# Two-layer pre-activation convolution: dense 3x3 stage, sixteen rounds behind it, seven chunk slots for x, two tile buffers

## What is computed

```
x = x + L0(groupnorm(x))      # layer 0
x = x + L1(groupnorm(x))      # layer 1

L0:  f    = relu(Wc @ x + bc)                        # 1x1, 512 -> 128 channels
     g    = relu(mean(x) @ Wc.T + bc) (x) Wkk + bkk  # 3x3 kernel from the means
     sk   = relu(Wc @ max over the 3x3 cells(x) + bc)
     dynW = relu(Wck[:, 0] * g + Wck[:, 1] * sk + bck)   # 128x128 channels, per image
     y    = conv3x3(f, dynW) + b_ad                  # 128 -> 128
     out  = Wf @ y + bf                              # 1x1, 128 -> 512 channels
L1:  grouped 3x3 convolution, 32 groups of 16 channels, no bias
```

## Time and profile before

| | us |
|---|---|
| device time, median of 3 runs | 3925.79 (3924.04 to 3929.71) |
| profiled execution, device time | 3910.82 |
| span of the profiled execution | 3909.1 |
| stage A of image 1 starts, of image 31 starts | 134.03, 3710.69 |
| mean granted TensorE clock | 0.970 |
| PE, DVE, ACT, POOL busy | 3543.0 (91%), 3003.4 (77%), 2177.4 (56%), 990.5 (25%) |
| DRAM traffic | 810.21 MB at 207 GB/s |

### The profile page before, as it was taken

One profiled execution on the slowest core, in us unless ns is written; L12 is line 12 of the kernel. 1 busy time (PEld: TensorE's weight loads), 2 busy tenths in 40 slices (PEclk: granted clock), 3 DMA queues, 4 the chain that ended last, 5 costly groups with the idle time before them and its releaser, 6 DMA issues.

```text
span 3909.1 us, 64944 instructions
## 1 busy us (share of the span) xinstructions
PE 3543.0 (91%) x18048; PEld 2728.8 (70%) x18048; DVE 3003.4 (77%) x8020; ACT 2177.4 (56%) x3911; POOL 990.5 (25%) x1036
## 2 busy tenths in 40 slices
PE   5799999999999999998999999999999999999996
PEld 4577776677776777766677767777666777667775
DVE  7788787778787878877787778787777877787853
ACT  4465555665555664556655556655566555566554
POOL 2131222322222322223222123222232131232223
PEclk9899999999999999999999999999999999999998
DMA  5778667777667786668776687866686776778646
GB/s 101 216 217 233 203 187 217 231 228 221 190 197 226 224 231 210 184 193 236 223 229 198 181 227 224 237 212 183 187 249 209 229 211 179 220 220 238 204 112 173
DMA packets 389593, 810.21 MB, mean 207 GB/s; under 512 B 67250, under 2 KB 297012, under 8 KB 376756
## 3 DMA queue, kind: packets, MB, share of 16 engines
q1 hardware_dynamic: 375220, 658.76, 61.2%
q10 hardware_dynamic: 14336, 151.00, 11.0%
HBM read 501.40 MB, written 308.28 MB: 207 GB/s over the span
## 4 chain that ended last, share of the span: by engine, by line
issue 65%; POOL 21%; PE 6%; DVE 3%; DMA 3%; SPq 1%; POOLq 1%; ACT 1%; ACTq 0%; DVEq 0%
POOL hl L410 21%; DMA tb<-x_rows 1%; PE pd L910 1%; PE pb L910 1%; PE pd L911 1%; PE pd L912 1%; PE pb L912 1%; PE pb L911 1%; POOLq L409 1%; DVE bst L636 1%; DVE mx L638 1%; DMA out<-tb 1%; DMA tb<-x 1%; DMA x_rows<-mrow 0%; PE pac L910 0%
## 5 line engine op out<-in xcount | busy, mean ns | idle before, releaser
L410 POOL TENSOR_TENSOR hl<-un,hl 128x384 f16<-128x384 f32 x1024 | 962.9, 942 | 2838.1 <-ACT hl L435 2838.0
L910 PE MATMUL pd<-hl,k_h 128*96 128x384 f16 x3072 | 1043.6, 340 | 220.0 <-POOL hl L410 135.5
L911 PE MATMUL pd<-hl,k_h 128*96 128x384 f16 x3072 | 1036.1, 337 | 0.0
L912 PE MATMUL pd<-hl,k_l 128*96 128x384 f16 x3072 | 1034.5, 337 | 0.0
L821 DVE SCALAR_TENSOR_TENSOR tb<-pd,kout,tb 96x384 f32<-96x384 f32 x1024 | 621.8, 607 | 327.7 <-PE pd L912 321.2
L431 ACT ACTIVATE un<-tb,b_t,s_t 128x384 f32<-128x384 f32 x1024 | 710.2, 694 | 153.8 <-DMA tb<-x_rows 147.1
L435 ACT ACTIVATE hl<-un 128x384 f16<-128x384 f32 x1024 | 538.8, 526 | 298.6 <-PE pd L912 269.5
L910 PEld LDWEIGHTS pd<-hl,k_h 128*96 128x96 f16 x3072 | 388.6, 126 | 418.7 <-issue 192.8
L810 DVE SCALAR_TENSOR_TENSOR x1b<-pac,bfc,xb 128x288 f32<-128x288 f32 (+2 forms) x1408 | 544.1, 430 | 81.9 <-PE pac L912 76.7
L478 ACT ACTIVATE xs<-pb,badc 128x480 fp32r<-128x480 f32 (+1 forms) x160 | 103.5, 647 | 846.0 <-PE pb L912 846.0
L910 PE MATMUL pb<-fh,dynh 128*128 128x480 f32 (+1 forms) x1440 | 553.3, 384 | 8.2 <-DVE dynl L715 8.2
(11 more groups left out here) (107 smaller groups left out, 4014.7 us busy)
## 6 DMA issues: line engine op xcount, KB each, us to landing
x_rows<-x1b SPq DMA_DIRECT2D x128, 1152.0 KB, 13.9
tb<-x_rows SPq DMA_DIRECT2D x128, 1152.0 KB, 9.6
out<-tb ACTq DMA_DIRECT2D x128, 1152.0 KB, 7.9
tb<-x SPq DMA_DIRECT2D x372, 384.0 KB, 9.7
xb<-x SPq DMA_DIRECT2D x124, 720.0 KB, 6.3
xb<-x SPq DMA_DIRECT2D x124, 432.0 KB, 10.6
tb<-x_rows SPq DMA_DIRECT2D x256, 192.0 KB, 10.7
x_rows<-mrow SPq DMA_DIRECT2D x64, 96.0 KB, 10.0
```

Of the source, the lines that this page charges most:

```text
L410: pool.tensor_tensor(hl[:, g % HL_RING, 1, :, 1:W + 1], un[:, g % U_RING], hl[:, g % HL_RING, 0, :, 1:W + 1], ALU.subtract).then_inc(hl_lo, 1)
L910: pe.matmul(acc, high_w, high_x, start=start, stop=False)
L911: pe.matmul(acc, high_w, low_x, start=False, stop=False)
L912: return pe.matmul(acc, low_w, high_x, start=False, stop=stop)
```

## The change

Stages B and C are taken apart. Per image TensorE runs A, then B without anything between its taps, then 16 rounds. A round is a pair of layer-1 groups of the preceding image (18 matmuls), and in rounds 0 to 5 four C units besides. C is cut otherwise: 24 units, chunk by chunk and row class by row class (a row class is the eight rows that lie six apart, 384 columns), so that x1 of a chunk is complete after six units. The residual has 24 operations, one for a unit. A pair's output is one DVE operation over two banks, 96 x 768; the pairs alternate between the banks pd and pb.

x has seven chunk slots: one for chunk 0, two for each other chunk. Each chunk of x is loaded once, whole; moments and maxima of chunks 1 to 3 are taken during B, of chunk 0 in rounds 3 to 5. x1b holds two chunks, so a chunk's x1 is written to DRAM before the chunk after next is made. tb has two slots, `T_SLOT = [0, 1, 0, 1]`: the load of chunk 2 waits for the store of chunk 0 of the same image, that of chunk 3 for the store of chunk 1. All DMAs, stores too, are issued by SP. ACT takes the squares of x1 in four operations of 2304 elements in place of 12, behind groups 7, 10, 13 and 16. The dynamic weights are made in rounds 13 and 14, with their high part at the end of the image and the low part in A. The loop's body is two images.

The diff, cut to its core:

```diff
-C_AFTER = (2, 4, 6, 8)
-D_FIRST = 13
-EARLY = 3
-LATE = {D_FIRST + 1: (0, 1), D_FIRST + 2: (2, 3)}
...
-AT_X_LOW = (28, 29, 30, 31)
-AT_SCALES = 6
...
-PREP_AT = (5, 6, 7, 8, 9, 11)
-PREP_IN_B = (4, 2)
-PREP_C = (0, 2, 3, 4, 3)
-PREP_FIRST = (0, 0, 1, 2, 3)
...
-STORE_AT = {20: 1, 28: 2}
-TAIL_STORE_AT = {12: 0, 20: 1}
+X_SLOTS = 7
+X1_SLOTS = 2
+T_SLOTS = 2
+T_SLOT = [0, 1, 0, 1]
...
+EARLY = {3: (0, 1), 4: (2, 3)}
+EARLY_GROUPS = 4
+AHEAD = XS_RING
+
+C_ROUNDS = 6
...
+STATS_IN_B = (1, 2, 3)
+STATS_LATE = (0,)
+SQUARE_AFTER = {7: 0, 10: 1, 13: 2, 16: 3}
+ROOT_AFTER = 22
+DYN_LOW_AT = 1
+SCALES_BEFORE = 2
+MOMENTS_AT = {3: (0, 0), 4: (0, 1)}
+MAXIMA_AT = {5: 0}
...
+PREP_MEANS_AT = 7
+PREP_VARIANCES_AT = 9
+PREP_SCALED_AT = 11
...
+def x_slot(c, odd):
+
+    return c if c < 1 else c + 3 * odd
...
+            def load_x(n, odd, c):
+                if isinstance(n, int) and n == 1 and c in STATS_IN_B:
+                    sp.wait_ge(max_done, Q)
+                    sp.wait_ge(k_lo, K_PARTS)
+                elif c in STATS_IN_B:
+                    reached(sp, x1_done, (n - 2) * CUNITS + (c + 1) * OR_)
+                sp.dma_start(xb[:, x_slot(c, odd), :], x_d[n, c]).then_inc(x_in[c], 16)
+            def write_x1(n, c):
+                dst, made = sc_w[n, c, :, :, AT:AT + BW], n * CUNITS + (c + 1) * OR_
+                sp.wait_ge(x1_done, made)
+                sp.dma_start(dst, x1b[:, c % X1_SLOTS]).then_inc(x1_out[c], 16)
...
-            def stage_x(n, pieces):
...
-                    stage_x(n + 1, range(STAGES + 2))
...
+                sp.wait_ge(x1_out[c], written)
...
+                if T_SLOT[c] in T_SLOT[:c]:
+                    sp.wait_ge(stored[T_SLOT.index(T_SLOT[c])], written)
+                else:
+                    reached(sp, stored[Q - 1 - T_SLOT[::-1].index(T_SLOT[c])], free)
...
+            def store(n, c):
+                dst, made = out[n, c], n * PAIRS + (c + 1) * PER_CHUNK
+                sp.wait_ge(out_done, made)
+                sp.dma_start(dst, t_slot(c)[0:M6].rearrange("p j b w -> p (j b w)")).then_inc(stored[c], 16)
...
+            def step(n, odd, d=True, more=True):
+                if d:
+                    if isinstance(n, int) and n == 1:
+                        sp.wait_ge(k_lo, K_PARTS)
+                    for c in range(2):
+                        load_t(n - 1, c)
                 if more:
+                    for c in STATS_IN_B:
+                        load_x(n + 1, 1 - odd, c)
+                for c in range(2):
+                    write_x1(n, c)
+                    if more and c in STATS_LATE:
+                        load_x(n + 1, 1 - odd, c)
+                if d:
+                    store(n - 1, 0)
+                write_x1(n, 2)
                 if d:
                     load_t(n - 1, 2)
+                write_x1(n, 3)
                 if d:
+                    store(n - 1, 1)
                     load_t(n - 1, 3)
                 write_means(n)
+                if d:
+                    store(n - 1, 2)
+                    store(n - 1, 3)
...
-            def store(n, c):
-                act.wait_ge(out_done, n * G + (c + 1) * GQ)
-                act.dma_start(out[n, c], t_slot(c)[0:M6].rearrange("p j b w -> p (j b w)")).then_inc(stored[c], 16)
...
+            def square(n, c):
+                act.wait_ge(x1_done, n * CUNITS + (c + 1) * OR_)
...
+                reached(act, sq_done, n * Q + c)
+                act.activation(fl[:, 1:H + 1, 1:W + 1], x1b[:, c % X1_SLOTS].rearrange("p k (b w) -> p (k b) w", w=W), ACT.Square,
+                               bias=cen[:, c:c + 1], accum_out=m2[:, c:c + 1]).then_inc(sq_done, 1)
             def root_first(n):
...
+                for g in range(EARLY_GROUPS, G):
+                    if d:
                         d_groups(n - 1, [g])
+                    if g in SQUARE_AFTER:
...
+            def residual(n, odd, u):
+                c, k = divmod(u, OR_)
+                if k == 0:
+                    if c < X1_SLOTS:
+                        reached(vec, x1_out[c + X1_SLOTS], n * 16)
+                        reached(vec, sq_done, n * Q)
+                    else:
+                        vec.wait_ge(x1_out[c - X1_SLOTS], (n + 1) * 16)
+                        vec.wait_ge(sq_done, n * Q + c - X1_SLOTS + 1)
+                vec.wait_ge(c_mm, n * CUNITS + u + 1)
+                vec.scalar_tensor_tensor(
+                    out=x1b[:, c % X1_SLOTS, k, :].rearrange("p (b w) -> p b w", w=W),
...
+                    in1=xb[:, x_slot(c, odd), :].rearrange("p (b k w) -> p k b w", k=OR_, w=W)[:, k],
...
...
+            def output(n, p):
+                vec.wait_ge(d_mm, n * G + 2 * (p + 1))
+                at = 2 * p % GQ
+                dst = t_slot(p // PER_CHUNK)[0:M6, at:at + 2].rearrange("p j b w -> p j (b w)")
+                vec.scalar_tensor_tensor(out=dst, in0=pair_banks(p)[0:M6, :, 0:BW], scalar=kout[0:M6, 2:3], in1=dst,
...
...
+                for r in range(PAIRS):
                     if d:
+                        output(n - 1, r)
+                    if r < C_ROUNDS:
+                        for u in range(r * C_PER_ROUND, (r + 1) * C_PER_ROUND):
+                            residual(n, odd, u)
+                    if more and r in MOMENTS_AT:
+                        c, part = MOMENTS_AT[r]
+                        moments(n + 1, 1 - odd, c, range(part * BANDS, (part + 1) * BANDS))
+                    if more and r in MAXIMA_AT:
+                        maxima(n + 1, 1 - odd, MAXIMA_AT[r])
+                    if r == X1_SUMS_AT:
                         x1_means(n)
+                    if r == X1_MEANS_AT:
                         x1_group_means(n)
                     if more:
+                        if r == PREP_MEANS_AT:
                             prep_means(n + 1)
+                        if r == PREP_VARIANCES_AT:
                             prep_variances(n + 1)
+                        if r == PREP_SCALED_AT:
+                            prep_scaled(n + 1, 0)
+                            prep_scaled(n + 1, 1)
+                        if r == PREP_SCALED_AT + 1:
+                            prep_scaled(n + 1, 2)
+                        if r == PREP_SCALED_AT + 2:
+                            dyn_inputs(n + 1)
+                            for part in DYN_HALVES:
+                                dyn_maxima(n + 1, part)
+                        if r == PREP_SCALED_AT + 3:
+                            for part in DYN_HALVES:
+                                dyn_global(n + 1, part)
+                if more:
+                    for i in range(AHEAD):
+                        x_low(n + 1, 1 - odd, i)
...
+            def c_unit(n, u):
+                c, k = divmod(u, OR_)
+                if u == 0:
+                    pe.wait_ge(y_lo, (n + 1) * NT)
+                if u >= C_BANKS:
+                    pe.wait_ge(x1_done, n * CUNITS + u - C_BANKS + 1)
+                three(pac[u % C_BANKS][:, 0:BW].rearrange("p (b w) -> p b w", w=W), wfh[:, c * P:(c + 1) * P], wfl[:, c * P:(c + 1) * P],
...
+            def d_pair(n, p):
+                reached(pe, out_done, n * PAIRS + p - 1)
+                for g in (2 * p, 2 * p + 1):
+                    pe.wait_ge(hl_lo, n * G + g + 1)
+                    acc = pair_banks(p)[0:M6, g % 2, 0:BW].rearrange("p (b w) -> p b w", w=W)
...
...
+                for r in range(PAIRS):
                     if d:
+                        if isinstance(n, int) and n == 1 and r == 0:
+                            pe.wait_ge(k_lo, K_PARTS)
+                        d_pair(n - 1, r)
+                    if r < C_ROUNDS:
+                        for u in range(r * C_PER_ROUND, (r + 1) * C_PER_ROUND):
+                            c_unit(n, u)
+                    if r == X1_MEANS_AT - 1:
                         x1_group_means(n)
+                    if more:
+                        if r == PREP_VARIANCES_AT - 1:
+                            group_mean(n + 1)
+                        if r == PREP_VARIANCES_AT:
+                            group_variance(n + 1)
+                        if r == PREP_SCALED_AT + 1:
+                            kernel_inputs(n + 1)
```

521 lines of the change are left out of this document (191 added, 330 removed).

## The result

The changed kernel takes **4108.82 us** (median of 4 runs, 4093.87 to 4124.97) against 3924.91 us before; the ratio is 1.0475, with a 95% interval of 1.0428 to 1.0522. The forecast was 4020 in a range of 3890 to 4145, so sign and range held, and about half of the loss was foreseen: +95 of +184 us. The profiled execution took 4124.97 us, at the upper end of its runs, and the one of before 3910.82 at the lower end of its own, so the two traces lie 214 us apart where the medians lie 184 apart. Differences per image that are read from these two traces are thus about 1 us larger than those of the medians.

The account below looks back on a forecast made before the run. TensorE sets the 119.2 us period; the changed order, with a slot's round trip deciding, gives 121.8, +78 us over 30 images, +18 at the head, 0 at the end: 4020 us after run-median allowance, range 3890 to 4145.

Parts of the forecast that it names:

- The round trip: Reuse of a tile slot: output, store, load, high and low part take 19.9 us, store and load alone 16.6.
- R1: Rival: slot's store plus load short, about 11 us, no wait at pair 12, median about 3848 us; chance 0.20.
- R2: Rival: slot's store plus load as long as under load, 19.9 us for 16.6, about 4120 us; chance 0.14.
- Where the wait lies: Second half of the rounds: TensorE idles 5 to 6 us ahead of pair 12, little ahead of pair 8.
- The wait for x1's means: Between pairs 6 and 7: TensorE waits 1.7 us for DVE's group means, between 0 and 3.0.
- The rounds: Rounds 0 to 5: 18 layer-1 matmuls and four C units take 5.1 us a round, 30.6 in all.
- The clock: TensorE's clock dips after the waits, costing 0.5 us more per image.
- The tail of DVE: Behind pair 13, ahead of A's x_low: outputs and dynamic weights' parts on DVE take 8.65 us.
- R3: Rival: DVE's tail slowed by POOL, more likely +2.8 us per image, about 4100 us; chance 0.10.
- The head: Image 0: loads of image 1's x wait for layer-1 weights and hold up B; +18 us, between 5 and 30.
- The end: After the last period: the same slot round trip without C, 0, plus or minus 5 us.
- R4: Rival: first-half waits (means, variances) and the head nearly nothing, period as before, 3915 to 3935 us; chance 0.08.

Follow-up runs that it names:

- The last experiment: Against the combined kernel at 3718.46 us: in rounds 0 to 5 two C units behind each group, two residuals ahead of the output; 3671.49 us.

## Why the prediction was right, and where it was not

Step by step, in us (measured: differences of medians over images 1 to 30 of the trace):

| step | forecast | measured | off by |
|---|---|---|---|
| B | 30.0 | 29.7 | -0.3 |
| rounds 0 to 5 | 30.6 | 32.4 | +1.8 |
| pair 6, x1's means, pair 7 | 8.1 | 7.1 | -1.0 |
| from there to pair 12 | 20.5 | 21.8 | +1.3 |
| pairs 12 and 13, inputs of the dynamic weights | 7.0 | 9.3 | +2.3 |
| pairs 14 and 15 | 6.0 | 5.8 | -0.2 |
| A | 19.6 | 19.3 | -0.3 |
| period | 121.8 | 125.4 | +3.6 |

That the time held within the range is in part luck: the errors of the terms have both signs, and the time lies near the upper end, where half of the loss was not foreseen. The trace of the changed kernel also lies 16 us above its median, so some 0.5 of the 3.6 may be this execution's.

**The round trip** was the right term, and for chunk 3 of the right size: 17.4 us in image 24 and 17.3 as a median for store and load, against 16.6. R1, whose point of decision was 13.4, is out with that. R2's 19.9 was not seen on chunk 3 (at most 18.0), but chunk 2's trip took 20.5, so in size R2 holds for that one. The Trainium skill, "DMA: Bandwidth & Descriptors", section "Anatomy of one DMA — SWDGE (gpsimd) path", has the fit by which the estimate was 10.3 us. It was made for another kind of queue; these runs show 17.3 on SP's queue, and the measurement decides.

**Where the wait lies** was wrong. I had chunk 2's load land "at 67 to 71, about when it's needed", and put 5 to 6 us ahead of pair 12. In image 24 it lands at 70.7, within those bounds, but pair 8 could have started at 69.1 and needs it 2.3 us earlier for the high and low part, at 66.8. So PE waits 3.9 us ahead of pair 8, and pair 8 with the mean's matmul takes 6.0 us on average in place of some 3.4, at a mean clock of 0.62 and with the square between its groups. By then chunk 3 is nearly back, and ahead of pair 12 little is left. From pair 7 to pair 12 it makes 21.8 against 20.5, by another path than the one that I had laid out. The runs with one reload left out show it: 90.3 and 91.0 for the two paths, 86.1 without both.

**The wait for x1's means** was put at 1.7 and takes 0.7; that gave 1.0 back and hides part of the other misses.

**The rounds** were mis-sized by 0.3 each, 1.8 per image, the largest term but one: I took C units back to back, when the fourth unit of a round waits for a bank that a residual must empty. The last experiment took it away. The residual had been priced at 0.55 and the output at 0.95; from start to start they take 0.54 and 0.93. That the residuals stand behind the output, and PE's banks with them, was what I had not followed. The output's group and the accumulator reads that each residual carries (line, engine, operation, count, busy and mean ns):

```profile
L779 DVE SCALAR_TENSOR_TENSOR big<-pb,kout,big 96x768 f32<-96x768 f32 x256 | 259.1, 1012 | 474.2 <-PE pb L871 474.2
L769 DVE DVE_READ_ACCUMULATOR x1b<-pac,bfc,big 128x1 f32 x768 | 60.8, 79 | 0.0
```

**The clock** was allowed 0.5 us per image behind all waits. Pair 8 at 0.53 and pairs 12 to 15 at 0.90 in the windows above took more. Behind pair 12 stands the wait for the inputs of the dynamic weights besides, 1.80 in the row at 3146.06, which I had taken as covered. That is the largest miss of the table, and the trace splits it: by means over images 1 to 30 pairs 12 and 13 with these inputs take 8.8 us where 7.0 was forecast. Of that 1.2 is the wait, and 0.7 the clock: pair 13 takes 3.6 us on average at a mean clock of 0.85, and 3.0 at 1.00 in the run without chunk 3's load.

**The tail of DVE** held: from the output of pair 13 to the first x_low 8.1 us in the trace against 8.65. R3 is out: nine operations take 2.43 us there, as in the earlier trace rows with POOL idle:

```profile
3156.59 2.43 DVE L664 SCALAR_TENSOR_TENSOR dtmp<-rows,gk,dtmp 128x128 f32<-128x128 f32 x9
...
3159.88 3.85 DVE L738 SCALAR_TENSOR_TENSOR xs<-big,negm,xs 128x480 fp32r<-128x480 f32 x6
```

**The head** held with its mechanism. In image 0 PE waits for y behind the moments of a chunk whose load had waited for POOL:

```profile
94.56 1.30 SPq L281 DMA_DIRECT2D big<-x  x3
...
105.79 0.74 PE L869 MATMUL pb<-fh,dynh 128*128 128x480 f32 x1 [23.66 <-DVE xs L755]
```

**The end** was put at 0 and took 13.6. The tail proper, which the prediction named as "the same round trip without C", is the smaller part of it. PE waits 18.0 and 9.7 us for tile loads there, and waited 14.0 and 8.7 before:

```profile
4053.47 0.52 PE L869 MATMUL pd<-hl,k_h 128*96 128x384 f16 x1 [18.03 <-POOL hl L398]
...
4089.57 0.52 PE L869 MATMUL pd<-hl,k_h 128*96 128x384 f16 x1 [9.68 <-POOL hl L398]
```

```profile
3842.58 0.56 PE L910 MATMUL pd<-hl,k_h 128*96 128x384 f16 x1 [13.98 <-POOL hl L410]
```

From the end of layer 0 of image 31 (4035.0, before 3823.7) to the end of the span it is 88.2 us against 85.3, so 2.8. The other 10.8 lie in the step of image 31 itself, from 3911.2 to 4035.0 against 3710.7 to 3823.7. That step isn't among the 30 periods, has both reloads of the slots (PE waits 4.7 and 2.1 us for them), and the prediction gave it no term. R4 did not happen: the wait for the variances was 1.8 against a forecast of 1.7, and the head cost its 19.

What was not tried: the two slots alone in the kernel before, and the earlier store without the smaller load.

## What to carry to other kernels

A buffer that is given back through a store needs its whole trip (last write, store, load, first use) in cover; lay the trip out from the last write, for each reuse, and ask which wait appears when the first one goes. Storing and loading in smaller pieces can replace a third buffer: halves took 5.5% off here. When two trips end at nearly the same point, removing either shows little or nothing, so a test that removes one and finds no gain has not cleared it. And a load queued behind a waiting one on the same queue inherits the wait.

## What the runs showed of the hardware

A 768-element output over two banks takes 1.01 us against 2 x 0.60 for two of 384, and 0.93 against 2 x 0.52 from start to start, so joining them saves a tenth to a sixth. Whole chunks of x (1152 KB) took 18.5 to 22.9 us to land when issued behind two tile loads, against 7.8 for chunk 0 (issued 3090.93, landed 3098.72 in image 24), which has only writes of x1 beside it. A tile load in three DMAs landed 11.3 us after its first issue, one of half the bytes after 6.2, while a store of half the bytes took 5.6 against 5.7. After 3.9 us without a matmul PE's clock was granted at 0.53 over the next 6.8 us; with matmuls on constants in the same wait it stayed at 1.00.
